# A fused decoder layer (attention, context attention, mixture of experts): how the gating logits are formed and where the routing stands

## The reference, cut to what matters

```
logits = x @ gate_w.T                        # N x 256 by 256 x 8
scores = sigmoid(logits);  scores_c = scores + correction_bias
grp = scores_c.reshape(N, 4, 2)              # keep 2 of 4 groups by their sums
choice = where(group kept, scores_c, 0)
topk_idx = top_k(choice, 4)[1]
topk_w = scores[topk_idx] / sum * 2.5        # cw: N x 8, zero where not chosen
g = x @ Wg[e];  u = x @ Wu[e]                # 256 x 128 for each e
y[e] = (silu(g) * u) @ Wd[e]                 # 128 x 256
out = sum_e y[e] * cw[e] + mlp_shared(x)
```

## Time and profile before

| | us |
|---|---|
| median of 3 runs | 662.88 (662.68 to 664.53) |
| the profiled execution | 661.01 |
| its span | 659.2 |
| TensorE busy | 641.9 (97%) |
| VectorE busy | 482.8 (73%) |
| ScalarE busy | 329.2 (50%) |
| GpSimd busy | 248.5 (38%) |

### The profile page before, as it was taken

The page is one execution under the profiler, slowest core; times in us unless marked ns, Lnnn a source line. Parts: engine busy times, 40 slices in busy tenths (PEclk is TensorE's granted clock), DMA queues, the critical chain, the costliest instruction groups (busy, mean ns, idle before and its releaser), DMA issues. The chain is left out here.

```text
span 659.2 us, 11928 instructions
## 1 busy us (share of the span) xinstructions
PE 641.9 (97%) x3912; PEld 549.3 (83%) x3912; DVE 482.8 (73%) x1279; ACT 329.2 (50%) x778; POOL 248.5 (38%) x321
## 2 busy tenths in 40 slices
PE   5999999999999999999999999999999999999997
PEld 3878888889788888897888777788888888888886
DVE  4788878878788688787888977776667766677433
ACT  4665675555756755557566363333433334334321
POOL 2256263353561734535634223233233232332221
PEclk9999999999999999999999999999999999999999
DMA  8534044051340441613614351413214032230400
GB/s 227 154 94 141 15 123 121 28 167 47 91 143 7 121 121 31 170 42 96 197 58 125 118 183 32 156 38 129 97 41 172 11 128 95 71 123 1 149 13 32
DMA packets 51806, 64.44 MB, mean 98 GB/s; under 512 B 3944, under 2 KB 49560, under 8 KB 50880
## 3 DMA queue, kind: packets, MB, share of 16 engines
q1 hardware_dynamic: 51776, 64.06, 31.9%
HBM read 56.60 MB, written 7.45 MB: 97 GB/s over the span
## 5 line engine op out<-in xcount | busy, mean ns | idle before, releaser
L1627 POOL TENSOR_TENSOR xt<-xt,cw_wide 128x512 f32<-128x512 f32 x55 | 73.2, 1331 | 173.4 <-ACT xt L1584 173.4
L1651 DVE TENSOR_TENSOR res<-bank,xt 128x512 f32<-128x512 f32 x62 | 42.6, 687 | 52.1 <-POOL xt L1627 47.5
L1588 ACT ACTIVATE a_hi<-res 128x512 fp32r<-128x512 f32 x42 | 26.6, 634 | 85.8 <-DVE res L1651 85.8
L75 PE MATMUL bank<-h_hi,w_lo 128*128 128x512 f32 x168 | 67.4, 401 | 0.1
L77 PE MATMUL bank<-h_hi,w_hi 128*128 128x512 f32 x168 | 66.1, 393 | 0.0
L76 PE MATMUL bank<-h_lo,w_hi 128*128 128x512 f32 x168 | 66.0, 393 | 0.0
L1656 DVE TENSOR_TENSOR a_lo<-res,a_hi 128x512 fp32r<-128x512 f32 x42 | 33.7, 803 | 22.4 <-ACT a_hi L1588 22.4
L1024 POOL TENSOR_TENSOR wz_lo<-tmp,wz_hi 128x512 fp32r<-128x512 f32 x28 | 35.0, 1281 | 37.6 <-DVE tmp L1195 37.6
L653 PE MATMUL bank<-ctxf,qg 125*112 125x256 f32 x192 | 46.7, 379 | 0.0
L640 PE MATMUL bank<-cw_wide,ctw 128*112 128x375 f32 x128 | 46.3, 483 | 0.2 <-ACT ctw L858 0.2
L1584 ACT ACTIVATE xt<-bank 128x512 f32<-128x512 f32 x61 | 36.0, 590 | 12.5 <-PE bank L77 12.3
(11 more groups left out here) (242 smaller groups left out, 2025.3 us busy)
## 6 DMA issues: line engine op xcount, KB each, us to landing
cw_wide<-in_ctx_t SPq DMA_DIRECT2D x32, 375.0 KB
ctxf<-in_ctx SPq DMA_DIRECT2D x32, 375.0 KB
cw_wide<-cw_scratch SPq DMA_DIRECT2D x7, 1536.0 KB, 8.0
xt<-in_x SPq DMA_DIRECT2D x8, 448.0 KB, 4.1
x_scratch<-x2b SPq DMA_DIRECT2D x8, 448.0 KB, 3.3
x2n<-x_scratch SPq DMA_DIRECT2D x7, 512.0 KB, 4.8
cw_wide<-cw_scratch SPq DMA_DIRECT2D x7, 512.0 KB, 4.4
x2t<-x_scratch SPq DMA_DIRECT2D x7, 512.0 KB, 3.9
```

The source lines that it names most:

```text
L75: pe.matmul(dst, a_lo, b_hi, start=first, stop=False, **kw)
L1588: act.activation(a_hi[n % (AHEAD + 1)][:, :], af[(p + n) % 2][:, :], ACT.Copy).then_inc(a_hi_ok, 1)
L1627: pool.tensor_tensor(sg[b][:, :], sg[b][:, :], cw_wide[p][:, ORDER[n], :], ALU.mult).then_inc(sgw_ok, 1)
L1651: dve.tensor_tensor(af[b][:, :], u_bank[b][:, :], sg[b][:, :], ALU.mult).then_inc(af_ok, 1)
```

## The change

The logits are formed the other way round: `logits` loads pieces of h3 (128 features by 128 tokens) and streams the 16 gate columns, which leaves tokens on partitions at once, in bank 7, 16 matmuls instead of four. `copy_logits`, `lgt`, `turn_logits` and their semaphores and waits go. In the expert stage the sum, exp and `route_groups` stand at n = 2 instead of 3, `route_ranks` at 3 instead of 4, `route_weights` at 4 instead of 5; in group 0 at 3, 4 and 4 instead of 4, 5 and 5. `logits` itself and `turn_cw` keep their places.

```diff
-        def logits(pe, g, h3_hi, h3_lo, b):
+        def logits(pe, g, h3_hi, h3_lo):
             pe.wait_ge(h3_lo_ok, KB * (g + 1))
-            for k in range(KB):
-                pe.matmul(b[0:2 * NEXP, :], gate[:, k, :], h3_lo[:, k, :], start=(k == 0), stop=False)
-                last = pe.matmul(b[0:2 * NEXP, :], gate[:, k, :], h3_hi[:, k, :], start=False, stop=(k == KB - 1))
+            for t in range(T):
+                dst, tok = h_bank[1][:, t * 2 * NEXP:(t + 1) * 2 * NEXP], slice(t * P, (t + 1) * P)
+                for k in range(KB):
+                    pe.matmul(dst, h3_lo[:, k, tok], gate[:, k, :], start=(k == 0), stop=False)
+                    last = pe.matmul(dst, h3_hi[:, k, tok], gate[:, k, :], start=False, stop=(k == KB - 1))
             last.then_inc(lg_mm, 1)
-
-        def copy_logits(act, g, b):
-            act.wait_ge(lg_mm, g + 1)
-            act.activation(lgt[:, :], b[0:2 * NEXP, :], ACT.Copy).then_inc(lgt_ok, 1)
-
-
-        def turn_logits(pe, g):
-            for t in range(T):
-                last = pe.transpose(h_bank[1][:, t * 2 * NEXP:(t + 1) * 2 * NEXP], lgt[:, t * P:(t + 1) * P],
-                                    ident[0:2 * NEXP, 0:2 * NEXP])
-            last.then_inc(t_lg, 1)
...
         def sum_logits(dve, g):
-            dve.wait_ge(t_lg, g + 1)
+            dve.wait_ge(lg_mm, g + 1)
...
@@ TensorE, attention stage, last group
-                        logits(pe, 0, h3_hi0, h3_lo0, h_bank[1])
+                        logits(pe, 0, h3_hi0, h3_lo0)
                     similarity(2)
-                    if last_group:
-                        pe.wait_ge(lgt_ok, 1)
-                        turn_logits(pe, 0)
@@ ScalarE, attention stage, last group
                     ct_copy(3)
-                    if last:
-                        copy_logits(act, 0, h_bank[1])
@@ TensorE, expert stage
-                        if not last:
-                            if n == 3 + late:
-                                pe.wait_ge(lgt_ok, g + 2)
...
                         if n == 2 + late and not last:
-                            logits(pe, g + 1, h3_hi[1 - p], h3_lo[1 - p], h_bank[0])
-                        if n == 3 + late and not last:
-                            turn_logits(pe, g + 1)
+                            logits(pe, g + 1, h3_hi[1 - p], h3_lo[1 - p])
@@ ScalarE, expert stage
                             if n == 2 + late:
-                                copy_logits(act, g + 1, h_bank[0])
-                            if n == 3 + late:
                                 exp_logits(act, g + 1)
@@ VectorE, expert stage
-                        if n == 3 + late and not last:
+                        if n == 2 + late and not last:
                             sum_logits(dve, g + 1)
                             route_groups(dve, g + 1)
-                        if n == 4 + late and not last:
+                        if n == 3 + late and not last:
                             route_ranks(dve, g + 1)
                             if late:
                                 route_weights(dve, g + 1)
-                        if n == 5 and not late and not last:
+                        if n == 4 and not late and not last:
                             route_weights(dve, g + 1)
```

More of the change, by code:

```diff
@@ L105, in decoder_layer @@
         tri8, tri4 = osb("tri8", [P, 8, 8]), osb("tri4", [P, 4, 4])
-        lgt = osb("lgt", [2 * NEXP, FFN_TOKENS])
         st3, mv3, r3a, r3 = osb("st3", [P, T, 6]), osb("mv3", [P, T, 2]), osb("r3a", [P, T]), osb("r3", [P, T])
@@ L113, in decoder_layer @@
         wk_in = osem("routing_constants_in")
-        lg_mm, lgt_ok = osem("logits_product"), osem("logits_copied")
-        t_lg, lg2_ok, lg_ok, eneg_ok = osem("logits_transposed"), osem("logits_halves"), osem("logits_ready"), osem("logits_exp")
+        lg_mm, lg2_ok, lg_ok, eneg_ok = osem("logits_product"), osem("logits_halves"), osem("logits_ready"), osem("logits_exp")
         route = osem("routing_step")
```

## The result

The changed kernel takes 664.96 us in the median of 15 runs (663.58 to 666.76), the kernel before 662.75 in as many runs at the same time (660.75 to 664.84). The ratio is 1.0032, interval 1.0018 to 1.0046: slower, by 2.1 us. In a second series it was 1.0020 (1.0005 to 1.0035). The forecast was 665.7 in a range from 662.4 to 668.4. Two executions, one of 1557 us (kernel before) and one of 2161 (`old_gating_ahead_spread`), are left out of all ratios.

A forecast was written before the change was run, and what follows sets the result against it. TensorE was taken to bound the kernel in the expert groups. Steady groups +1.3, group 0 +1.3 and attention stage +0.2 gave +2.8 us on the median of 662.88: 665.7 us, range 662.4 to 668.4.

The forecast's parts named there:

- steady groups: Expert-stage groups 1 to 5: new gating 0.26 us dearer in each, no waits from moved routing, +1.3 us in all.
- group 0: First expert-stage group: wait at turn_cw goes, a longer one of some 2.6 us comes at gate_up(7), +1.3 us.
- attention stage: Last attention group: gating 1.75 instead of 1.49 us and the copy wait, at most 0.3 later; +0.2 us taken.
- TensorE's price of the new gating: On TensorE, 16 load-bound matmuls cost 1.68 us plus 0.07 for leaving, 1.75 against 1.49 for the old gating.
- Rival A: New logits matmuls: fp32r load half hidden, 0.052 us a pair, 0.90 for 16; sum -1.7, 661.2 us; chance 0.10.
- Rival C: New logits matmuls: a pair costs 0.118 us, 2.03 per group with the exit; sum +4.3, 667.2 us; chance 0.12.
- Rival B: Group 0: product(5) comes in time, no stall at gate_up(7), group gains 1.6 us; sum -0.1, 662.8 us; chance 0.13.
- Rival D: Groups 1 to 5 stall too, slack at gate_up(8) used up, 0.5 to 1 us each; 668.2 to 670.7 us; chance 0.10.
- ScalarE's copies: ScalarE's copy of the 16x512 logits goes, seven times; its removal was costed at nothing.

The follow-up runs named there:

- old_gating_ahead_spread: Kernel before with old logits products, copy and turn, routing one expert ahead, and group 0's route_weights at expert 5: 662.98 us, ratio 0.9989.
- old_gating_ahead: Changed kernel with the old logits products, copy and turn put back at expert 2, routing still one expert ahead: 663.91 us, ratio 0.9998 to the kernel before.
- spread_group0: Changed kernel with route_weights of group 0 at expert 5 instead of behind route_ranks at expert 4: 664.37 us, ratio 1.0008 to the kernel before.
- gate_only: Changed kernel with the new logits products but sum, exp and routing at their old places: 668.02 us, ratio 1.0073 to the kernel before.
- double_logits: Changed kernel with every logits product made twice in one run, 32 pairs in place of 16: 684.96 us, ratio 1.0330 to the kernel before.
- again: The changed kernel run again without any edit: 664.09 us against 662.83 for the kernel before, ratio 1.0020.
- gate_only_late: Changed kernel with routing at its old places and, in steady groups, the logits products behind gate_up(3): 665.15 us, ratio 1.0019 to the kernel before.

## Why the prediction was right or wrong

The direction held and the time, 664.96, is 0.7 from 665.7. In the traces, though, the change is worth 1.1 us, not 2.8; the rest of the measured 2.1 goes with how often either kernel had which pace near the start, which the prediction didn't know. It landed so near by luck, by two errors of opposite sign: 1.7 too much for the change, and some 1.0 for the start that it didn't have. The terms, forecast and measured: steady groups +1.3 and +1.16 (0.83 + 0.33), group 0 +1.3 and -0.05, attention stage +0.2 and -0.02. Step by step:

**TensorE's price of the new gating: right, 0.05 low.** Taken 1.75, measured 1.80 by difference and 1.81 by doubling. The load is what is paid: 0.111 a pair, a little above the 0.104 and 0.106 of the rows used. A steady group was to grow by 0.26 and grew by 0.21 (0.83 over four). The slots before were worth 1.49 by experts' differences, so 0.31 was due, and 0.30 is what `old_gating_ahead` shows; the missing 0.1 is what the moved routing gains at `turn_h3`, which the prediction didn't have. So its 0.26 lies near 0.21 by two small errors as well. The rows used are fp32, and in the trace each fp32 matmul, transpositions aside, stands as two records of load and product (four matmuls of L539 in the program, eight records; 128 of L613, 256 records), each fp32r one as one (16 of each gating): the prediction counted records, and so its price for a load could be carried over. Rival A, the hidden load, falls: it needed a pair below 0.088, and the new loads are recorded at 191 and 192 ns, as long as the rest. The Trainium skill, "TensorE: Matmul & The Clock Gate", Weight-path perf modes, lets a fast weight load take place for 128 weights of a type that is not FP32, and since it reads 32 bits at a time it notes no win for fp32. The trace can't tell whether fp32r takes it, but shows that fp32r gains nothing: 191 and 192 ns beside fp32's 192. Rival C's 0.118 a pair is about as far from 0.111 as the forecast's 0.105, but its price for the 16 is the wrong one: sixteen at 0.118 are 1.89, with the exit of 0.07 1.96, while the prediction has 1.96 with the exit hidden and 2.03 with it. By 1.96 the rival's sum would be some +4.0 and not +4.3; neither is seen.

**Group 0: the mechanism right, the term mis-sized.** product(5) came 6.97 us behind product(4), as reckoned, gate_up(7) waited 2.43 us (forecast some 2.6), and gate_up(8) started 1.11 later by the traces' common clock (410.56 - 3.23 against 406.22; forecast 1.33). What failed is the step that ended there and took 1.3 us for the whole of group 0. The kernel before has a further wait, 0.97 us at `turn_h3` of group 1, released by h3 on VectorE,

```profile
420.06 1.09 PE L162 MATMUL bank<-ident,h 128*128 128x128 f32 x8 [0.97 <-DVE h L202]
```

and this wait goes when routing ends earlier. The last `down` ahead of this turn takes 2.56 us in the kernel before and 1.43 in the changed one, so 1.13 come back there, and group 0 costs nothing: 40.30 us against 40.35. The view behind the earlier trace rows lists that wait, equally long, on a line of its own, and the prediction took one of its lines as the only one that concerns the routing. Its sum was stopped at the first place where both traces could be compared and not at the next place where TensorE must wait for VectorE. Rival B, that the stall at gate_up(7) doesn't come, falls, and the 1.6 us that it gave group 0 aren't seen. Spreading the routing of group 0 (`spread_group0`) makes the wait at `turn_h3` come back as the stall shrinks, so both belong to the same surplus of VectorE's work.

**Steady groups: right in the number, wrong in the reason.** In the changed kernel "the slots alone count" held. But the prediction measured the slack at gate_up(8), 1.1 us, and gave the move of the routing no worth in these groups. The tight place was `turn_h3`, where h3 was ready 0.06 us ahead of the turn and held TensorE up by 0.1 in the mean. New products at the old routing cost 0.9 a group (`gate_only`); the two halves of the change are not independent, and the second pays for the first. Rival D (VectorE as the bound of the steady groups) was right that the steady groups were tight before and named the wrong place; in the changed kernel itself no wait of TensorE is listed in a steady group.

**Attention stage: right in size at first.** +0.27 at its second `turn_h3`; at the start of the expert stage the two traces are again 3.22 apart (379.71 and 382.93), so nothing of it remained, as the prediction had held possible; +0.2 was forecast. Where it was absorbed wasn't traced. ScalarE's copies brought nothing, as costed.

## What to carry to other kernels

Turning a product round saves the copy and the turn of its result, but each 128x128 piece of the long operand becomes a weight load that is paid in full (0.11 us) when only 16 columns follow: count loads, 16 against 4. A step moved on another engine is to be followed to every later place where TensorE can wait for it, not to the first: the place without slack (`turn_h3`) came behind the one whose slack was measured (1.1 us at gate_up(8)). And compare traces from a common point behind the start, or a change of 1 us drowns in a difference of 3.

## What the runs showed of the hardware that I had not expected

Of the seven runs of 32 matmuls that load 128x128 and stream 16 columns (`double_logits`, 3.49 us each in the expert stage, TensorE busy all the time), six went with a fall of the granted clock to 0.50, the 1.2 GHz of its two levels. It lasted some 3.4 us in the expert stage, where it began 0.1 to 0.8 us behind the end of the run, and nearly 7 in the attention stage, where it began within the run (at 348.9, the run being 346.01 to 350.03). The seventh, in group 1, was followed by none. Runs of 16 (1.7 us) were followed by none in any trace, even two in a group, with 1.00 throughout. In groups 2 to 5 of `double_logits` the fall cost 1.5 to 1.6 us beside the 1.8 of the products, in the attention stage some 3.3. Such a run isn't the only occasion: the clock also fell to 0.50 at 383.5 to 386.9 us in `again` and at 386.4 to 389.8 in `double_logits`, ahead of that group's products and shortly behind the 1.7 and 2.2 us in which TensorE does nothing between the stages, while the other traces have such a gap and no fall. What decides it is not shown.

Near the start of the kernel the matmuls of the changed kernel's execution ran at about half pace up to 19.4 us, though the profile gives the granted clock there as 1.00:

```profile
12.70:19.40 6.70, 6.70 (x22) 5.32 (x21) 3.28 (x8) 3.58 (x8) 0.00 (x0) 1.00 0.76 182
```

Their spacing, 0.43 us, is that which `double_logits` shows at 0.50. In `gate_only_late` like matmuls near the start stand 0.43 apart too, and there the record gives 0.50:

```profile
14.00:17.00 3.00, 3.00 (x9) 2.13 (x8) 0.30 (x2) 1.57 (x3) 0.00 (x0) 0.50 0.91 216
```

That makes a lower clock without a record of it the likelier reading of the changed kernel's start; that nothing else held the matmuls back is not shown.
